# A node pass of a four-layer graph network: the first norm behind the attention layers computed on ScalarE, its mean formed directly, and the row-map transfers spread over the stages in another way

## What is computed

```python
h = jnp.maximum(_layernorm(x, axis=-1), 0.0)
x = x + _L0_gnn_ref(h, edge_index, edge_attr_16, ...)   # five attention layers
h = jnp.maximum(_layernorm(x, axis=-1), 0.0)
x = x + _L1_gnn_ref(h, edge_index, edge_type_2, ...)    # typed attention: a * out + (1 - a) * h, a = sigmoid(skip)
h = jnp.maximum(_layernorm(x, axis=-1), 0.0)
x = x + _L2_gnn_ref(h, edge_index, ...)                 # convolution with degrees, gelu
h = jnp.maximum(_layernorm(x, axis=-1), 0.0)
x = x + _L3_gnn_ref(h, edge_index, edge_type_4, ...)    # four edge types: sums + h @ W[0] + bias
```

## Time and profile before

| | |
|---|---|
| median of 3 runs | 5280.24 us (5279.77 to 5292.36) |
| span of the profiled execution | 5284.5 us |
| TensorE busy | 4281.1 us (81%) |
| VectorE busy | 4007.8 us (76%) |
| ScalarE busy | 3358.8 us (64%) |
| GpSimd busy | 3254.8 us (62%) |
| mean granted TensorE clock | 0.880 of full speed |

### The profile page before, as it was taken

The page is one execution under the profiler, slowest core; times in us unless marked ns, Lnnn a source line. Parts: engine busy times, 40 slices in busy tenths (PEclk is TensorE's granted clock), DMA queues, the critical chain, the costliest instruction groups (busy, mean ns, idle before and its releaser), DMA issues. The chain is left out here.

```text
span 5284.5 us, 101919 instructions
## 1 busy us (share of the span) xinstructions
PE 4281.1 (81%) x28013; PEld 3707.5 (70%) x28013; DVE 4007.8 (76%) x15157; ACT 3358.8 (64%) x9065; POOL 3254.8 (62%) x2905
## 2 busy tenths in 40 slices
PE   4899999999976978969969958776895858869575
PEld 4777777778865867858858847644775847757475
DVE  5799999999976766767757767787676959859765
ACT  2788887888855866847847847643873537758400
POOL 2888888878877727637457367222761257566277
PEclk6999999999988989989989979855997979989755
DMA  3999876665645636636636546487773759847332
GB/s 92 187 219 217 220 218 212 222 219 206 212 150 125 143 85 133 135 77 142 128 90 141 110 107 142 110 246 225 169 153 90 196 141 248 236 114 132 74 94 85
DMA packets 1107280, 825.56 MB, mean 156 GB/s; under 512 B 209510, under 2 KB 1068202, under 8 KB 1106396
## 3 DMA queue, kind: packets, MB, share of 16 engines
q1 hardware_dynamic: 1026800, 690.47, 48.7%
q0 software_dynamic: 77040, 128.08, 12.0%
q10 hardware_dynamic: 2880, 0.50, 0.1%
HBM read 374.78 MB, written 448.11 MB: 156 GB/s over the span
## 5 line engine op out<-in xcount | busy, mean ns | idle before, releaser
L805 POOL DMA_INDIRECT gat_G<-table,k_src_row x980 | 1071.7, 1094 | 316.6 <-issue 282.5
L1598 ACT ACTIVATE gat_Gw<-gat_G,gat_al 128x128 f32<-128x128 f32 x1960 | 618.5, 395 | 89.0 <-DVE gat_al L1423 89.0
L1454 DVE SCALAR_TENSOR_TENSOR gat_Gw<-gat_own,gat_al,gat_Gw 128x128 f32<-128x128 f32 x1960 | 555.3, 344 | 70.5 <-ACT gat_Gw L1598 70.3
L1715 PE MATMUL gat_psG<-gat_ends_at,gat_Gw 128*128 128x128 f32 x3920 | 536.4, 281 | 42.3 <-DVE gat_Gw L1454 42.2
L1743 PE MATMUL gat_psZ<-gat_aggT,t_gat_wh 128*128 128x256 f32 x1960 | 525.5, 391 | 16.5 <-ACT gat_hT L1624 16.1
L1715 PEld LDWEIGHTS gat_psG<-gat_ends_at,gat_Gw 128*128 128x128 f32 x3920 | 491.9, 197 | 53.3 <-DVE gat_Gw L1454 50.1
L635 PEld LDWEIGHTS nodes_psR<-t_ident_v,nodes_hTl 128*128 128x128 f32 x3168 | 435.3, 193 | 106.0 <-issue 1.8
L635 PE MATMUL nodes_psR<-t_ident_v,nodes_hTl 128*128 128x132 f32 x3168 | 450.5, 279 | 0.0
L479 POOL TENSOR_TENSOR nodes_rstd<-nodes_var,k_half 128x14 f32<-128x14 f32 x140 | 367.7, 2626 | 116.0 <-DVE nodes_var L546 116.0
L1624 ACT ACTIVATE gat_hT<-gat_psZ,t_gat_bias 128x256 f32<-128x256 f32 x490 | 231.6, 473 | 266.4 <-PE gat_psZ L1744 263.4
L1743 PEld LDWEIGHTS gat_psZ<-gat_aggT,t_gat_wh 128*128 128x128 f32 x1960 | 338.6, 193 | 57.9 <-ACT gat_aggT L1605 18.7
(11 more groups left out here) (668 smaller groups left out, 12635.5 us busy)
## 6 DMA issues: line engine op xcount, KB each, us to landing
table<-nodes_rows SPq DMA_DIRECT2D x660, 198.0 KB
table<-nodes_n SPq DMA_DIRECT2D x396, 192.0 KB
gat_own<-table SPq DMA_DIRECT2D x490, 132.0 KB
table<-gat_rows SPq DMA_DIRECT2D x392, 132.0 KB
nodes_x<-in_x SPq DMA_DIRECT2D x132, 192.0 KB
out<-nodes_x_out SPq DMA_DIRECT2D x132, 192.0 KB
gat_G<-table,k_src_row POOLq DMA_INDIRECT x980
hgt_q<-enter_q SPq DMA_DIRECT2D x98, 144.0 KB, 2.2
```

The lines of the kernel that those rows point to most:

```text
L805: eng.indirect_dma_start(to, None, table, bass.IndirectOffsetOnAxis(ap=index, axis=0)).then_inc(sem, 16)
L1454: ins = eng.scalar_tensor_tensor(Gw[:, i % RS, t, h, :], own[:, i % RO, t, 0:D], al[:, g % 2, 1, a:a + 1], Gw[:, i % RS, t, h, :], ALU.mul ...
L1598: ins = eng.activation(Gw[:, i % RS, t, h, :], G[:, i % RG, t, 0:D], ACT.Copy, scale=al[:, g % 2, 0, a:a + 1])
L1715: mm = eng.matmul(o[:, h * P:(h + 1) * P], Gw[:, i % RS, t, h, :], ends_at[:, i % RE, t, :], start=True, stop=True)
```

## The change

Three edits, all in the node pass:

1. The norm n1 is computed on ScalarE, with `Identity`, scale `rstd` and bias `shift`, in front of the gated copy, in place of `normed` on VectorE. VectorE's sum x1 now waits for the norm of the block two before (its buffer), and `shift` is computed in four more stages.
2. The mean is formed as 0.5 x diff + mean1 in one operation, in place of `total` and `negmean`; the norms subtract it, and `shift` is mean x -1 x rstd.
3. The 392 row-map transfers: five in two stages while there are slots (245 in k below 98), then four a stage until k = 134.

```diff
-        negmean, var, rstd = (A.sb(m, [P, 4, M]) for m in ("negmean", "var", "rstd"))
+        mean, var, rstd = (A.sb(m, [P, 4, M]) for m in ("mean", "var", "rstd"))
...
-                per = (len(steps) + N - 1) // N
+                early = NS * 5 // 2
+                due = [min(len(steps), 5 * k // 2 if k <= NS else early + 4 * (k - NS)) for k in range(LAST + 2)]
...
-                    for what, c in steps[k * per:(k + 1) * per]:
+                    for what, c in steps[due[k]:due[k + 1]]:
...
-                        ins = eng.tensor_scalar(to[:, t, 0:D], of[:, t, :], negmean[:, k % 4, at + t:at + t + 1],
-                                                rstd[:, k % 4, at + t:at + t + 1], ALU.add, ALU.mult)
+                        ins = eng.tensor_scalar(to[:, t, 0:D], of[:, t, :], mean[:, k % 4, at + t:at + t + 1],
+                                                rstd[:, k % 4, at + t:at + t + 1], ALU.subtract, ALU.mult)
...
-                        eng.tensor_tensor(total[:, :], mean0, mean1, ALU.add).then_inc(s.small, 1)
                         eng.wait_ge(s.small, n_small + 1)
                         eng.scalar_tensor_tensor(spread2[:, :], diff[:, :], 0.25, diff[:, :], ALU.mult, ALU.mult).then_inc(s.small, 1)
+                        eng.scalar_tensor_tensor(mean[:, k % 4, :], diff[:, :], 0.5, mean1, ALU.mult, ALU.add).then_inc(s.small, 1)
                         eng.wait_ge(s.small, n_small + 3)
-                        eng.tensor_scalar(negmean[:, k % 4, :], total[:, :], -0.5, None, ALU.mult).then_inc(s.small, 1)
-                        eng.wait_ge(s.small, n_small + 4)
...
                         eng.wait_ge(s.xb, b + 1)
+                        if b >= 2:
+                            eng.wait_ge(s.nB1, b - 1)
                         eng.tensor_tensor(x1[:, b % 2, :, :], wide(psX), xb[:, b % XB, :, :], ALU.add).then_inc(s.x1, 1)
...
-                    if is_block(k):
-                        eng.tensor_tensor(shift[:, k % 4, :], negmean[:, k % 4, :], rstd[:, k % 4, :], ALU.mult).then_inc(s.shift, 1)
-                    b = k - 4
-                    if is_block(b):
-                        if b >= RB:
-                            eng.wait_ge(st5[b % RB], 16 * (b // RB))
-                        normed(k, n1[:, b % RB, :, :], x1[:, b % 2, :, :], at_1, T, s.nB1)
+                    if k < N + 4:
+                        eng.scalar_tensor_tensor(shift[:, k % 4, :], mean[:, k % 4, :], -1.0, rstd[:, k % 4, :], ALU.mult, ALU.mult
+                                                 ).then_inc(s.shift, 1)
...
                     if is_block(c):
+                        eng.wait_ge(s.shift, k + 1)
+                        if c >= RB:
+                            eng.wait_ge(st5[c % RB], 16 * (c // RB))
+                        for t in range(T):
+                            ins = eng.activation(n1[:, c % RB, t, :], x1[:, c % 2, t, :], ACT.Identity,
+                                                 bias=shift[:, k % 4, at_1 + t:at_1 + t + 1],
+                                                 scale=rstd[:, k % 4, at_1 + t:at_1 + t + 1])
+                        ins.then_inc(s.nB1, 1)
                         eng.wait_ge(s.nB1, c + 1)
                         eng.activation(h5c[:, c % 2, :, :], n1[:, c % RB, :, :], ACT.Relu, scale=K.hgt_gate[:, 1:2]
```

More of the change, by code:

```diff
@@ L347, in node_pass @@
         st = A.sb("st", [P, 2, M, 6])
-        diff, total, spread2, square = (A.sb(m, [P, M]) for m in ("diff", "total", "spread2", "square"))
-        negmean, var, rstd = (A.sb(m, [P, 4, M]) for m in ("negmean", "var", "rstd"))
+        diff, spread2, square = (A.sb(m, [P, M]) for m in ("diff", "spread2", "square"))
+        mean, var, rstd = (A.sb(m, [P, 4, M]) for m in ("mean", "var", "rstd"))
         shift = A.sb("shift", [P, 4, M])
@@ L539, in _ @@
                         eng.scalar_tensor_tensor(square[:, :], sq0, float(D) * LN_EPS, sq1, ALU.add, ALU.add).then_inc(s.small, 1)
-                        eng.tensor_tensor(total[:, :], mean0, mean1, ALU.add).then_inc(s.small, 1)
                         eng.wait_ge(s.small, n_small + 1)
                         eng.scalar_tensor_tensor(spread2[:, :], diff[:, :], 0.25, diff[:, :], ALU.mult, ALU.mult).then_inc(s.small, 1)
+                        eng.scalar_tensor_tensor(mean[:, k % 4, :], diff[:, :], 0.5, mean1, ALU.mult, ALU.add).then_inc(s.small, 1)
                         eng.wait_ge(s.small, n_small + 3)
-                        eng.tensor_scalar(negmean[:, k % 4, :], total[:, :], -0.5, None, ALU.mult).then_inc(s.small, 1)
-                        eng.wait_ge(s.small, n_small + 4)
                         eng.scalar_tensor_tensor(var[:, k % 4, :], square[:, :], 1.0 / D, spread2[:, :], ALU.mult, ALU.add
                                                  ).then_inc(s.var, 1)
-                        n_small += 5
+                        n_small += 4
                     b = k - 3
```

## The result

The changed kernel takes **5442.44 us** (median of 4 runs, 5440.8 to 5451.71) against 5284.98 us for the kernel before, timed beside it on the same chip: ratio 1.0306, 95% interval 1.0287 to 1.0326 (the quotient of the two medians, 1.0298, lies inside it). The forecast was 5451, 3.2% slower. The span of the profiled execution is 5441.1 us, 156.6 more than the earlier trace rows. The power that GpSimd computes once in each stage, line 479 before, is L480 now.

The account below looks back on a forecast made before the run. It took a ScalarE-TensorE loop without slack, with a GpSimd-VectorE loop at 11.03 us setting stages with slots. Terms 108.7 + 9 + 3.9 + 38 + 1.5 - 3 + 13 = 171 on 5280 gave 5451 us, range 5410 to 5500.

Parts of the forecast that it names:

- The ring: ScalarE between the copied scores and h5c: three norms plus handover add 1.31 us a stage, nothing hides it.
- ring one: Loop of ScalarE (scores to hT7) and TensorE (to next scores): 10.95 us with slots, 9.55 without, becoming 12.26 and 10.86.
- -21 and +19: Forecast's own bounds for the norm on ScalarE: 1.15 to 1.51 us a stage over some 126 stages.
- Rival 1: Node pass: ring two binds and the move frees it; sum -6, 5274 us, not slower; chance 5%.
- ring two: Loop of GpSimd (power, gathers, transfers, xb) and VectorE's small operations: 11.03 us with slots, no longer binding after the change.
- Rival 2: TensorE's clock falls more often as it waits: 5489 us at one stage in four, 5610 in every; chance 13%.
- Rival 3: Norm costs less without slots, using TensorE's 1.5% idle time, and the end hides its reads: 5425 us; chance 9%.
- 83 x 1.31 = 108.7: Stages with slots: the norm's added time on ScalarE, 1.31 us in each of 83 stages, 108.7 in all.
- +13: End, k = 132 to 134: 11 reads beside pieces of dinv make GpSimd need 39.1 us instead of 26.1.
- 13 to 14 us named as a sign: Sign that the forecast is right: two stages of this length at the end of the node pass.
- Booked at nothing: GpSimd and VectorE: new mean, 2.5 transfers with slots, four reads without slots; no time booked, +5 kept for the range.
- 10.8 at most: Stages without slots: ring two's length in us with four reads, against ring one's 10.86.

Follow-up runs that it names:

- spare_tight: Kernel before plus three spare ACTIVATEs a stage on ScalarE, behind the wait for the scores, right ahead of h5c: 5425.03 us, ratio 1.0225.
- spare_scalar: Kernel before plus the same three spare ACTIVATEs a stage on ScalarE, ahead of the wait for the scores: 5345.4 us, ratio 1.012.
- spare_vector: Changed kernel plus three more norms a stage on VectorE, written to a buffer nobody reads: 5444.69 us, ratio 1.0313.
- norm_only: Kernel before with only the norm n1 moved to ScalarE ahead of h5c; old mean and row map: 5435.94 us, ratio 1.0283.
- rowmap_only: Kernel before with only the row-map transfers spread as in the change: 5325.27 us, ratio 1.0075.
- norm_back: Changed kernel with the norm n1 put back on VectorE, new mean and row map kept: 5319.25 us, ratio 1.0061.
- mean_only: Kernel before with only the mean formed directly, norm n1 still on VectorE, old row map: 5280.38 us, ratio 0.9987.
- rows_on_vector: Kernel before with mean formed directly, xb issued right behind the power, and layer 4's row copy moved from ScalarE to VectorE: 5278.75 us, ratio 0.9995.

## Why the prediction was right

**The ring.** The step that carries the forecast, three ACTIVATEs of 1.26 and a handover between L748 and h5c with nothing to hide them, was right in every part: 12.23 for ring one with slots (12.26 forecast), 10.85 without (10.86), the handover 0.03 in place of 0.05. `spare_tight` shows that the place does it without any change of the data flow, `spare_scalar` that the same load of ScalarE elsewhere costs about half as much, and `spare_vector` that VectorE's load does nothing in these stages. The prediction's bounds for the step are 1.14 and 1.46 where it derives them and 1.15 and 1.51 where it forms the range; its -21 and +19 follow from the former.

**Rival 1** (ring two binds and the move frees it) fell with `spare_vector` and `norm_only`. The Trainium skill (Perfetto Trace Analysis, Identifying the Most-Contended Engine) would have one work on the engine of highest occupancy; VectorE had 91% here beside ScalarE's 81%, and moving the norm to ScalarE alone made the kernel 2.8% slower (`norm_only`). The measurement decides: occupancy didn't say where the slack was, single stages did.

**Rival 2** (the clock falls more often) was wrong in its direction. The prediction weighed that TensorE would idle longer, and it does, 1.67 us in each stage with slots and 1.49 without; yet between 200 and 1500 us the clock falls twice where it fell seven times before. What the prediction held against the rival is in the rows: the idle time stands behind full products, and the stops of ring two behind the products of four columns are gone. Which of the two counts for more wasn't tested.

**Rival 3** (the norm costs less without slots, and the end hides its reads) did not come true: these 29 stages pay 1.29 each, 37.3 in all, and the end pays 9.

**The sum was 14 us too high.** Two terms were mis-sized. First, 83 x 1.31 = 108.7 was added to the measured 11.04 of before, though the text had found ring one at 10.95 and said that it becomes 12.26: the step from 11.04 to 12.26 is 1.22, so 101.3, and 101.4 was measured. The 0.08 of ring two, with its stops, disappears under a longer ring one and shouldn't have been carried over. That the corrected figure agrees to 0.1 is luck: ring one itself is 12.23, which gives 98.8, and the two falls of the clock with the longer stages around them, which the sum hadn't booked, bring 2.7. Secondly, a read at the end was priced at 1.68 (the mean of the earlier trace rows, 1.41, with 0.27 of idle time). Nine of the eleven take 0.94 to 1.01 and two 1.29, with up to 0.30 of idle time ahead of each, about 1.30 a read, so the three stages cost +9.0 in place of +13, and none took the 13 to 14 us named as a sign. The mean of the earlier trace rows was made of two kinds of reads: 59 of the 87 take 0.96 to 1.07, and 28, each the third of its stage, 2.28 to 2.38. The prediction had taken the price of a read as given, but it hangs on what VectorE does beside it. With n1 on VectorE its three sums come later in the stage, and the third read starts in the first of them also at the end. The same third read in the same stage, in the changed kernel and in `spare_vector`:

```profile
1686.42 1.29 POOL L810 DMA_INDIRECT k_src_row<-row_of,first_src_tm  x1 [0.30 <-issue]
...
1688.26 2.06 POOL L816 DMA_INDIRECT k_src_row<-row_of,first_src_tm  x1 [0.30 <-issue]
```

In `rowmap_only` and `norm_back`, which have the norm on VectorE too, the three stages take 37.7, close to the +13. So the lower price came with the move of the norm, which the prediction didn't see. The rest, -1.9 between k = 130 and 132 and -1.2 behind 135, is small.

**Booked at nothing, and rightly so**: the mean (`mean_only`), 2.5 transfers in place of 3 with slots (`rowmap_only`: 11.00), and the four reads without slots, in the changed kernel. But the last was right only because the norm moved. The prediction's "10.8 at most" for ring two held (10.55 in `rowmap_only`, a stage that binds when ring one is 9.55), which also means that the row map costs 0.6 to 0.75% where the norm stays on VectorE (`norm_back`, `rowmap_only`).

## What to carry to other kernels

Ask of a move not which engine is fuller but whether the instruction lands between a wait and the signal that closes a loop of two in-order queues; if no idle time is noted in that piece, its whole length, with the handover, is paid in every stage. When the bound changes, start the sum from the new bound, not from the old stage plus the addition, and don't add up parts that were measured one by one. Take the price of a transfer from the place where it will stand: a mean over issues beside a busy and an idle neighbour fits neither, and the change may move the neighbour too.

## What the hardware showed that was not expected

- GpSimd's issue of an indirect transfer is held back by VectorE's sums of two inputs in SBUF, and by how much depends on where it starts. In the kernel before, from k = 15 to 135, the 33 issues that start in the first of the three sums take 1.82 to 2.38 us and the 78 that start in the third take 1.25 to 1.29, while all those that start beside VectorE's one-input norms or statistics take 0.95 to 1.11. The 20 that start beside z6, a sum with one input in PSUM, take 0.97 to 0.98. In `rows_on_vector` the 114 that start in the second sum take 1.80 to 1.89. The Trainium skill (SBUF — State Buffer, Who interferes with whom) infers that `tensor_tensor` doesn't hold up the writing of descriptors; these rows speak against that for this form of transfer. Why the third read of `rowmap_only` outlasts the sums by 0.8 us wasn't tested.
- An ACTIVATE that reads what its predecessor on the same engine wrote starts 0.03 us after its end (1257.76 to 1257.79), against an overlap of 0.09 where nothing is read from the predecessor (L772 starts at 1258.31, h5c ends at 1258.40). In this pair a dependence within ScalarE costs 0.12 us. `norm_only` against `spare_tight` shows 0.14 to 0.16 a stage for the whole of it (medians of 12.24 and 12.09 with slots, 10.85 and 10.69 without), the norms' own waits and operands included.
- Length alone doesn't tell which idle time of TensorE the clock falls behind. In the kernel before, from k = 15 to 130, TensorE stands idle for 0.67 us or more 18 times, each time behind products of four columns and in front of `turn`; the clock fell to 0.50 behind five of them, 0.90 to 1.58 us long, and not behind others of 0.93 and 1.26. In the changed kernel there are 115 such idle times in the same stages, each behind products of full width: the two with a fall are 1.92 and 1.94 long, two more of 1.91 and 1.92 have none, and neither have the many of 1.67 and 1.49. `spare_tight`, with 1.52 or 1.53 in 81 of the 83 stages with slots, has no fall there.
